# Graph layer kernel on Trainium2: degrees as a second product with the places in the count loop, five sets of one-hots, three place registers per batch

## What is computed

```python
ones = jnp.ones(src.shape[0])
out_deg = segment_sum(ones, src, num_segments=N)
norm_out = clip(out_deg, 1.0, None) ** (-0.5)
for _ in range(3):
    msg = (x * norm_out[:, None])[src]
    agg = segment_sum(msg, dst, num_segments=N)
    x = 0.5 * (agg * norm_in[:, None]) + 0.5 * h0
```

## Time and profile before

| what | us |
|---|---|
| median of 3 runs | 1170.32 |
| lowest and highest of them | 1169.7 and 1171.43 |
| the profiled execution, its own time | 1174.88 |
| its span, first to last instruction | 1173.1 |

### The profile page before, as it was taken

One profiled execution on the slowest core, in us unless ns is written; L12 is line 12 of the kernel. 1 busy time (PEld: TensorE's weight loads), 2 busy tenths in 40 slices (PEclk: granted clock), 3 DMA queues, 4 the chain that ended last, 5 costly groups with the idle time before them and its releaser, 6 DMA issues.

```text
span 1173.1 us, 33827 instructions
## 1 busy us (share of the span) xinstructions
PE 955.8 (81%) x11293; PEld 789.2 (67%) x11294; DVE 984.7 (84%) x2684; ACT 608.5 (52%) x1511; POOL 602.5 (51%) x745
## 2 busy tenths in 40 slices
PE   3666666668888998989947999999999998899960
PEld 2666666657667887777825777888777777677750
DVE  7988888879999999777637999999898888788866
ACT  7555555541110000122236878788777777677765
POOL 2000000024676444466577677777777777777711
PEclk8999999979988999999968999999999999999975
DMA  3000000000000000011147677777766776676601
GB/s 98 1 0 0 0 0 0 1 1 2 2 2 3 3 3 3 20 35 43 49 128 218 194 211 217 218 213 217 222 200 207 204 209 199 191 222 198 200 15 56
DMA packets 77515, 117.43 MB, mean 100 GB/s; under 512 B 20488, under 2 KB 38972, under 8 KB 77372
## 3 DMA queue, kind: packets, MB, share of 16 engines
q1 hardware_dynamic: 58172, 63.13, 18.0%
q0 software_dynamic: 19200, 52.45, 15.9%
HBM read 108.66 MB, written 6.86 MB: 98 GB/s over the span
## 4 chain that ended last, share of the span: by engine, by line
DVE 32%; PE 26%; POOL 21%; issue 13%; ACT 4%; DMA 2%; SPq 1%; DVEq 1%; POOLq 0%; ACTq 0%
POOL region L937 13%; PE bank L1795 6%; DVE stage L1043 5%; POOL U L937 5%; PE bank L1680 5%; DVE aggT L1226 2%; PE bank L1682 2%; DVE stage L1206 2%; DVE stage L1219 2%; PE bank L1892 2%; POOL stage L937 2%; DVE aggT L1043 2%; PE bank L1917 1%; PE bank L1904 1%; PE bank L1756 1%
## 5 line engine op out<-in xcount | busy, mean ns | idle before, releaser
L937 POOL DMA_INDIRECT region<-src_split,region x272 | 265.0, 974 | 86.3 <-issue 81.5
L1795 PE MATMUL bank<-U,region 128*128 128x256 f16 (+1 forms) x1875 | 244.2, 282 | 6.6 <-DVE U L1310 3.8
L1795 PEld LDWEIGHTS bank<-U,region 128*128 128x128 fp8e4 x1875 | 184.0, 101 | 43.0 <-DVE U L1310 4.3
L2181 ACT CAST region<-bank 128x512 f16<-128x512 f32 x338 | 180.7, 591 | 0.0
L2059 ACT CAST region<-bank 128x500 f32 x202 | 119.9, 594 | 92.1 <-PE bank L1682 68.1
L2161 ACT ACTIVATE region<-bank 128x512 f16<-128x512 f32 x169 | 100.9, 597 | 63.9 <-PE bank L1895 58.3
L1680 PE MATMUL bank<-stage 128*128 128x175 f16 x544 | 92.1, 254 | 49.1 <-DVE aggT L1043 25.8
L1467 DVE SCALAR_TENSOR_TENSOR region<-bank,region 128x512 f16<-128x512 f32 x169 | 116.4, 689 | 12.8 <-ACT region L2161 9.9
L826 POOL TENSOR_TENSOR aggT<-stage 128x520 f16<-128x520 f16 x52 | 76.2, 1485 | 93.7 <-DVE stage L1203 84.1
L1892 PE MATMUL bank<-region,xs 128*128 128x256 f16 x676 | 104.2, 278 | 20.8 <-DVE region L1467 13.5
L1451 DVE TENSOR_SCALAR region<-region,stage 128x512 f16<-128x512 f16 x338 | 109.6, 366 | 12.5 <-DMA region<-slot_rows 12.5
(11 more groups left out here) (292 smaller groups left out, 2350.8 us busy)
## 6 DMA issues: line engine op xcount, KB each, us to landing
region<-slot_rows SPq DMA_DIRECT2D x169, 256.0 KB
region<-in_dst_dram SPq DMA_DIRECT2D x100, 64.0 KB
region<-src_split,region POOLq DMA_INDIRECT x272
slot_rows<-aggT SPq DMA_DIRECT2D x104, 3.2 KB
src_split<-U SPq DMA_DIRECT2D x25, 64.0 KB, 1.6
src_split<-xs SPq DMA_DIRECT2D x25, 64.0 KB, 1.5
tgt_split<-q SPq DMA_DIRECT2D x25, 64.0 KB, 1.6
region<-tgt_split SPq DMA_DIRECT2D x100, 16.0 KB
```

The source lines that it names most:

```text
L937: nc.gpsimd.indirect_dma_start(out=rows_of(n, i), out_offset=None, in_=src_split, in_offset=bass.IndirectOffsetOnAxis(ap=listed[n % LISTS] ...
L1795: z = nc.tensor.matmul(bank[2 * (k % 2) + p][:, 0:width], count[:, h, b * P:(b + 1) * P], U[k % 2][:, h, 0:width], start=h == 0, stop=h == ...
L2181: nc.scalar.copy(y_rows[u % 4][:, a, :], bank[3 + a][:, :]).then_inc(rows_copied, 1)
```

## The change

- The degrees come from a product with `L` as weights and `M` as moving operand, 175 columns, into `bank[4]`; the 7 columns of each `high` are summed by one DVE reduction after the loop. The `H` one-hots, their zeroing on POOL, the wait for them on PE, the copy to `outsum` and its transpose are gone.
- Since the sets are smaller, five fit: two and one in the places of before, two more in `hx_words`. So `over_groups` writes 10 groups out, runs a loop with 10 groups in its body 9 times, and writes the last one out.
- The first tile of a batch always has place 0, so only the other three are kept, in `places`: a load takes 12 words instead of 16, and the first tile's address is a constant.

```diff
-    DEEP = 3
+    DEEP = 5
+    MOVED = TPB - 1
...
-        offi = sb("offi", [1, T], i32)
+        places = sb("places", [1, NBAT * MOVED], i32)
...
-        stage_words = (GT * MW + 2 * GT * P + 2 * NB * KW) // 2
-        stage = sb("stage", [P, (DEEP - 1) * stage_words], f32)
+        stage_words = (GT * MW + GT * P + 2 * NB * KW) // 2
+        stage = sb("stage", [P, GT * MW + 2 * GT * P + 2 * NB * KW], f32)
+        one_hots = ((stage, 0), (stage, stage_words), (aggT, TB * P), (hx_words, 0), (hx_words, stage_words))
...
-            for h in range(DEEP):
-                nc.gpsimd.memset(H[h][:, :, NB:P, :], 0.0).then_inc(upper_zeroed, 1)
...
-            nc.vector.tensor_copy(offi[0:1, :], offs[0:1, :])
+            nc.vector.tensor_copy(places[0:1, :].rearrange("p (b t) -> p b t", t=MOVED), by_batch(offs)[0:1, :, 1:TPB])
...
-                one_hot(H[h][:, :, 0:NB, :], high[:, here], NB, GT // 2).then_inc(high_ready, 1)
...
-            nc.vector.tensor_copy(outsum[:, :], bank[4][:, 0:P]).then_inc(outdeg_ready, 1)
-            dve.wait_ge(outsum_turned, 1)
-            nc.vector.tensor_scalar_max(deg[:, :], bank[5][:, 0:NB], 1.0).then_inc(outdeg_ready, 1)
+            nc.vector.tensor_reduce(deg[:, :], bank[4][:, 0:MW].rearrange("p (h j) -> p h j", j=TW),
+                                    mybir.AxisListType.X, ALU.add).then_inc(outdeg_ready, 1)
+            dve.wait_ge(outdeg_ready, 1)
+            nc.vector.tensor_scalar_max(deg[:, :], deg[:, :], 1.0).then_inc(outdeg_ready, 1)
...
-            pe.wait_ge(upper_zeroed, DEEP)
...
-                    at[0] = load_row(ET.PE, offi, g * GT, OFF_MAX, min(2 * GT, T))
+                    at[0] = load_row(ET.PE, places, g * 2 * MOVED, OFF_MAX, 4 * MOVED)
...
-                pe.wait_ge(high_ready, g + 1)
...
-                        to = at[0][i % 2 * GT + c * TPB + k]
+                        to = at[0][(i % 2 * 2 + c) * MOVED + k - 1] if k else 0
...
-                        z = nc.tensor.matmul(bank[4][:, 0:P], H[h][:, a, :, t], L[h][:, a, :, t],
+                        z = nc.tensor.matmul(bank[4][:, 0:MW], L[h][:, a, :, t], M[h][:, a, :, t],
                                              start=begin and k == 0, stop=end and k == TPB - 1)
...
-            pe.wait_ge(outdeg_ready, 1)
-            nc.tensor.transpose(bank[5][:, 0:P], outsum[:, :], ident[:, :]).then_inc(outsum_turned, 1)
```

More of the change, by code:

```diff
@@ L258, in gnn_kernel @@
         signs = sb("signs", [P, 1], f16)
-        stage_words = (GT * MW + 2 * GT * P + 2 * NB * KW) // 2
-        stage = sb("stage", [P, (DEEP - 1) * stage_words], f32)
-        M, L, H, K = [], [], [], []
-        for i in range(DEEP):
-            block, taken = (stage, [i * stage_words]) if i < DEEP - 1 else (aggT, [TB * P])
+        stage_words = (GT * MW + GT * P + 2 * NB * KW) // 2
+        stage = sb("stage", [P, GT * MW + 2 * GT * P + 2 * NB * KW], f32)
+        one_hots = ((stage, 0), (stage, stage_words), (aggT, TB * P), (hx_words, 0), (hx_words, stage_words))
+        M, L, K = [], [], []
+        for block, first in one_hots:
+            taken = [first]
             M.append(carve(block, taken, [GT // 2, MW, 2], f16))
             L.append(carve(block, taken, [GT // 2, P, 2], f16))
-            H.append(carve(block, taken, [GT // 2, P, 2], f16))
             K.append(carve(block, taken, [NB * KW, 2], f16))
-        assert taken[0] <= NPAD
+            assert taken[0] <= block.shape[1]
+        assert len(one_hots) == DEEP
         taken = [0]
@@ L296, in gnn_kernel @@
         starts = carve(stage, taken, [HALF_BLOCKS], i32)
-        assert taken[0] <= (DEEP - 1) * stage_words
+        assert taken[0] <= stage.shape[1]
         taken = [0]
@@ L322, in gnn_kernel @@
         part_rows = carve(u0_words, taken, [TB * P])
-        outsum = sb("outsum", [P, P], f32)
         deg = sb("deg", [P, NB], f32)
@@ L382, in gnn_kernel @@
         code_ready = sem("code_ready")
-        high_ready = sem("high_ready")
         pass_ready = sem("pass_ready")
@@ L387, in gnn_kernel @@
         banks_set = sem("banks_set")
-        upper_zeroed = sem("upper_zeroed")
-        outsum_turned = sem("outsum_turned")
+        upper_set = sem("upper_set")
+        tiles_turned = sem("tiles_turned")
         pads_cleared = sem("pads_cleared")
@@ L781, in _ @@
                                     base=0, pattern=[[-1, P]], channel_multiplier=1).then_inc(consts_set, 1)
-            for h in range(DEEP):
-                nc.gpsimd.memset(H[h][:, :, NB:P, :], 0.0).then_inc(upper_zeroed, 1)
             g.wait_ge(colf_ready, 5 * len(HALVES))
-            nc.gpsimd.memset(U[0][:, :, 2 * D:2 * D + 2], UNIT).then_inc(upper_zeroed, 1)
+            nc.gpsimd.memset(U[0][:, :, 2 * D:2 * D + 2], UNIT).then_inc(upper_set, 1)
             g.wait_ge(count_copied, BATCHES)
@@ L1177, in _ @@
             dve.wait_ge(x_loaded, 32)
-            dve.wait_ge(upper_zeroed, DEEP + 1)
+            dve.wait_ge(upper_set, 1)
             def low_part(g):
@@ L1191, in _ @@
             low_part(len(GROUPS) - 1)
-            dve.wait_ge(outsum_turned, 2)
+            dve.wait_ge(tiles_turned, 1)
             link(nc.vector.tensor_scalar(starts_f[0:1, :], bank[6][0:1, 0:HALF_BLOCKS], -1.0, 0.0, ALU.add, ALU.max))
@@ L1696, in _ @@
             over_groups(pe, counts)
-            pe.wait_ge(outdeg_ready, 1)
-            nc.tensor.transpose(bank[5][:, 0:P], outsum[:, :], ident[:, :]).then_inc(outsum_turned, 1)
             pe.wait_ge(starts_ready, 1)
             nc.tensor.matmul(bank[6][0:1, 0:P], tiles_before[:, :], ident[:, :], start=True, stop=True)\
-              .then_inc(outsum_turned, 1)
+              .then_inc(tiles_turned, 1)
             SLOTS = ((NB // 12, 2, 3), (2 * NB // 5, 0, 1), (3 * NB // 4, 3, 3), (NB - 2, 1, 1))
```

## The result

| | before | after |
|---|---|---|
| time, median (range) | 1170.41 us (1169.7 to 1171.43), 4 runs | 1136.38 us (1132.37 to 1136.56), 4 runs |
| profiled execution / its span | 1174.88 / 1173.1 us | 1132.37 / 1130.4 us |
| last load of places starts | 237.6 us | 201.1 us |
| start of the last product with an offset | 240.00 us | 203.31 us |

The changed kernel takes 0.9693 of the time of the one before, with a 95% interval of 0.9676 to 0.971: 34 us less. Forecast were 22.2 less, 1148.1, with a range from 1142: the direction was right and the gain too small by a third. Measured again beside the experiments, the changed kernel took 1137.22 us (1134.44 to 1139.22, 5 runs), 0.9699 [0.9674, 0.9724].

The account below looks back on a forecast made before the run. PE's sequencer was taken to bound the count loop. Load -13.6, address steps -6.5, branches -2.4, second product +0.5, first product not waiting for `high` -0.2: -22.2 us, giving 1148.1 us, range 1142 to 1162.

Parts of the forecast that it names:

- The bound: Count loop: PE's own sequencer holds PE, and DVE waits for PE; 4.07 us per ordinary pair of groups.
- The load: PE's register load of places, once per pair: 12 words instead of 16 take 0.84 instead of 1.105 us, gaining 13.6 us.
- The address steps: PE's sequencer in the count loop: one step per batch goes, 202 x 0.037 = 7.5 us, taken as 6.5.
- the wait that moved: PE's wait for `low_ready`, on 101 address steps before, now on the product itself; lowers that gain to between 3.7 and 7.5.
- The branches: Count loop: 15 turns become 9, so 6 branches at 0.4 go, gaining 2.4 us.
- The product with the places: Second product, 47 more columns on 808 tiles: hidden within the loop, showing only at both ends, +0.5 us.
- DVE, ACT and behind the loop: DVE 3.16 us per pair, still waiting for PE; ACT at most 3.3, below 3.67; work behind the loop changes by 0.
- costs and gains nothing: DVE's `high` one-hots, 17 us in all, covered by waits for PE; they count only if PE needs under 3.16 per pair.
- The load got shorter: Rival on PE's load of places: 12 words cost what 16 do, 13.6 us are lost, 1161.7 us; chance 0.08.
- the array was not in the way: Rival in the count loop: loads wait until the array's queue is nearly empty, pairs stay at 4.07, 1166 us; chance 0.06.
- The longer body was not fetched again: Rival in the count loop: each turn fetches two or three instruction packets, kernel slower, +31 us and 1179; chance 0.05.
- faster still: Rival on PE's load: 0.6 us or less, until DVE's 3.16 per pair is the bound, 23 us at most, 1125; chance 0.05.

Follow-up runs that it names:

- the first: The changed kernel with the places part undone: 16-word loads and the first tile's address from a register again; 1169.16 us, 0.9973 of before.
- second: The changed kernel with each batch's first tile taking its address from a register, still 12-word loads; count ends 22.3 us later, whole time (69345 us) no measure.
- sixth experiment: The changed kernel without the second product, out-degrees taken as 1; 1134.66 us, 0.9675 of before.
- the last experiment: The changed kernel with one PE wait per group for the one-hots and one for ACT's copy; 1125.14 us, 0.9607 of before.

## Why the prediction was wrong

**The bound** was right: the sequencer, not DVE and not the array, in spite of what the page's shares and the releasers in the timeline suggest. The start times show it, and the first, second and sixth experiments confirm it: four of a batch's nine products less change the count by 1.4 us, one step per batch more by 22.

**The load**, 13.6 forecast, was 12.9 to 13.0. The line from 4 to 16 words held (12 words 0.849), and with it the answer to the Trainium skill (Runtime: NRT & Kernel Launch, Instruction fetch mechanics), which gives about 200 ns per register: 16 words less 12 are 64 ns a word here.

**The address steps are the step that failed.** The prediction took 202 x 0.037 = 7.5 us, lowered to 6.5 for the wait that moved; measured are 22.3. The earlier trace rows give a duration, and it was taken for the price. But the starts of two neighbouring steps are 0.115 us apart, so 0.078 of each step stand in no row. The Trainium skill has the reason to expect such a thing, in Perfetto Trace Analysis, Per-instruction lifecycle: what the profiler-reported window actually captures: of an operation that the sequencer does alone only the execution is reported; fetch and decode come ahead of that window, and the wait and the spreading of the semaphore, which it calls the "hidden tail", are outside too. The trace agrees that time is missing, 0.037 shown and 0.110 paid; which of these parts it is no run here tells. The load was priced well by its duration because only its length changed: one load of a pair stayed, and so did the gap of 0.058 behind it. The address step went whole, with its gap, which is two thirds of its price. A sum over the pair would have shown it: the load and sixteen steps are 1.105 + 16 x 0.037 = 1.70 of 4.07 us by their rows, and 2.4 us had no name. By the start times (medians) the load takes 1.163, the sixteen steps 1.840 and the pair's nine other steps 0.963, together 3.97 of the 4.07; the rest are gaps longer than usual.

**The branches** were right (2.4 forecast, 2.5 measured). The product with the places was forecast at +0.5; leaving it out altogether gave 1.4 (the sixth experiment). The count closes with these: 12.9 + 22.3 + 2.5 - 1.4 = 36.3 against 36.7 measured, where 1.4 is an upper bound of what the wider product costs, since part of it was there before the change too.

**DVE, ACT and behind the loop** came out as forecast: 3.16 per pair for DVE, still waiting for PE, 0 behind the loop. That a saving on DVE "costs and gains nothing" would have held at the forecast pace of 3.67. At the real one it was worth 1.6 us. The prediction named PE below 3.16 as the condition; but whether taking `high` away pays depends on what DVE needs with it, 3.49, and the changed kernel's PE is below that.

**The rivals.** The load got shorter and the array was not in the way. The longer body was not fetched again: from 40 to 195 us the queue for instructions moved

```profile
q8 instruction: 3, 0.05, 0.1%
```

in the changed kernel, three packets in 9 turns where two or three per turn would have been needed, and a pair behind a branch is 0.42 us longer by the starts of the loads, where it was 0.35 before. The Trainium skill (Runtime: NRT & Kernel Launch, Instruction fetch mechanics) has a memory of 2048 instructions for PE at the head of that section, and further on the stall at a target outside two pages. The trace agrees with the first as far as a body of 465 goes. It shows no such stall, but doesn't refute the rule, since where the body lies against those pages is not known. The rival "faster still" gave the right direction from the wrong cause, a cheaper load. Its end of 1125 was reckoned with DVE as the bound; the last experiment came to 1125.14 by taking waits away, with DVE close to that bound, and that the two numbers agree so well is partly luck.

**The range** took its low end from the load alone (0.72 us). The steps were not in it: an error of three times in their price was outside of what the prediction had bounded, although the gap behind a step was there in the start times. With the bounds 0.037 and 0.115 for a step the sum would have reached from -22 to -38 and the range down to 1132.

What stays open: why the stages behind the count differ by up to 6 us between executions of kernels that are the same there, what the sequencer does in the gap, and why some gaps are 0.03 us longer than the others.

## What to carry to other kernels

In a loop with dynamic addresses, price the steps of an engine's sequencer by the distance between their starts, not by the duration of their rows; and if the engine rests while its data are ready, fill that rest with its sequencer's loads, steps, waits and branches before blaming the releaser that the timeline names. A constant address, taking out a wait that another implies, and a shorter load are then worth more than a product less, which here brought 1.4 us at most. But check what each removal lengthens: packing the words traded a load for steps that cost more, and a merged wait came so early that the sequencer stood in it.

## What was not expected of the hardware

- A step of PE's sequencer costs its duration plus a gap: 0.078 us behind address steps of 0.037 and of 0.075 to 0.126 alike, 0.058 behind a load. Added steps of 0.032 to 0.037 cost 0.110 each.
- How many products and weight loads stand in between makes no difference to the sequencer: some 560 of each fewer in 120 us, at the same pace within 1%. That some do stand there lengthens the gap by 0.02 (0.055 and 0.075 behind the same step).
- Address arithmetic has a duration by kind: 0.032 or 0.037 for a plain step, 0.075 to 0.126 for one with a division or a remainder.
- A load of registers takes 0.306 for 1 word, 0.331 for 4, 0.849 for 12 and 1.105 for 16: nearly flat up to 4 and then 0.065 per word.
